# Scatter order of a weight table's tail, the place of TensorE's register loads in three look-ups, and the order of VectorE's score sums

## The chip, the cores and the metric

The program runs on one core of a Trainium2 chip. The metric is the device time of one execution in microseconds (us). Before the change three runs gave a median of 3548.18 us (3548.17 to 3554.03).

## The reference

Four graph layers over 3,125 nodes of 256 features and 50,000 edges, sorted by destination, each followed by a residual and a layer norm:

```python
edge_index = jnp.stack([src, dst])
x = _layernorm(x + _L0_gnn_ref(x, src, dst, edge_weight, ...))
x = _layernorm(x + _L1_gnn_ref(x, ..., edge_attr_3, edge_index))
x = _layernorm(x + _L2_gnn_ref(x, edge_index, ...))
x = _layernorm(x + _L3_gnn_ref(x, src, dst, ...))
```

What the change touches are two of their parts. In L0 the neighbours are summed with the edge weights, and in L1 (and the two attention layers inside L2) every edge gets a score from its two nodes:

```python
gathered = edge_weight[:, None] * x[edge_col]                        # L0
neigh = segment_sum(gathered, edge_row, num_segments=N_NODES)
...
alpha = einsum(h_src, a_src) + einsum(h_dst, a_dst)                  # L1, 8 heads of 32
enc = relu(edge_attr @ edge_W.T + edge_b).reshape(-1, H, D)
alpha = alpha + sum(enc * h_dst, axis=-1)
...
e = alpha_s[src] + alpha_d[dst]                                      # L2, 4 heads, twice
```

L3 (three dense-table sums of neighbours, each with two projections and batch norms) isn't touched.

## The kernel before

**Tiling.** The edges stand in 392 tiles of 128 (391 with edges, `EDGES_T`), four tiles to a quad, 98 quads. The nodes stand in 25 tiles of 128, and `S` = 416 steps pair an edge tile with a node tile, since a tile of sorted edges can reach over a boundary.

**First stage, to about 640 us.** L0's sum is made as a dense product. For every edge tile VectorE sums weights and counts of equal (source, destination) cells (`summed`, L2061), and GpSimd writes them into a table `t_w` in device memory with one indirect DMA for each edge tile (`weight_sums`, L803, the scatter at L817). Rows of the table are destination nodes, so row tile t is complete when the quads up to some number, read from the data into `need_i`, have landed. With some 16 edge tiles to a row tile that number is 84 for row tile 20, 88 for 21, 92 for 22, 96 for 23 and 98 for 24. The order of the scatters is `w_order` (L382): groups of eight quads, in each group first tile 0 of all its quads, then tile 1, and so on; the last group has ten quads, 88 to 97. Two scatters of the same quad must not be in flight together, so each one waits until the one eight before it has landed (`written`, L393; eight semaphores, `moved` and `gath`, in turn). As GpSimd passes such a wait it raises `w_landed` by the quads that are complete (`quads_by`, L386), and after the last scatter it waits for all that is left and raises the rest.

SyncE reads the table back, two row tiles at a time (a pair, 13 pairs), each in a left and a right half, into a ring of four buffers in SBUF: `complete` (L585) waits for `w_landed` of that row tile, L608 issues the load, and the buffer has to be free, which TensorE's `w_out` tells. TensorE turns the counts (L993) and multiplies the weights with the nodes' features (L1018); VectorE adds the pairs (L2421).

**The look-ups.** In three layers (k = 0 for L1 and k = 1, 2 for the two attention layers) TensorE's `look_up` (L1138) makes, for four steps a turn and four turns a lap, the edge's source terms by one-hot products (L1159, L1169) and the target terms by one-hot products with the table of one node tile (L1180 for k = 0, L1182 else). Which node tile belongs to a step is known only from the data: it stands in `tn_i` and is loaded into 16 registers once a lap (`tiles_at`, L1133, the load at L1135), behind the source products of turn 0. For k = 0 TensorE also makes the products of the edges' attributes (L1151), which ScalarE passes through relu (L1535); for each turn VectorE's `of_edges` (L2183) takes the maximum over the source terms, which are all but one strongly negative (L2190), copies the targets' own term (L2195), multiplies the attributes with the targets' features (L2196) and sums (L2201). A first look-up runs from about 700 to 1134 us, the second from 1631 to 1785, the third from 2228 to 2398. Beside them GpSimd gathers rows of the nodes' features (L853, L900) and puts some aside (L874); behind each, `add_up` (L1251) sums these rows with the weights (L1259), which VectorE accumulates (L2344).

Of the kernel before, what the change touches and what calls it, by code (L numbers as in the profile page):

```python
# [6 lines left out]
P = 128  # L7
N = 3125
NT = 25
# [4 lines left out]
S = ET + NT - 1  # L14
SB, SQ = 4, 104
UN, HU = 16, 8
# [24 lines left out]
D = 256  # L41
# [16 lines left out]
PIECES = WT // 2  # L58
W_GROUP = 8
HALF_W = 12 * P  # L60
STAGED = [range(0, 6), range(6, 12), range(12, 18), range(18, NT)]
# [22 lines left out]
def build(nc, a):  # L84

    with ExitStack() as ctx:
# [60 lines left out]
        drel = sb("drel", [P, S])  # L147
        tn_i = sb("tn_i", [P, S], I32)
        te_i = sb("te_i", [SQ, SB], I32)
# [231 lines left out]
        w_groups.append(range(W_GROUP * len(w_groups), QUADS))  # L381
        w_order = [L0H * q + b for quads in w_groups for b in range(L0H) for q in quads if L0H * q + b < EDGES_T]  # L382
        w_first = [min(n for n, j in enumerate(w_order) if j // L0H == quads[0]) for quads in w_groups]
        quads_by = []
        for n in range(len(w_order)):
# [4 lines left out]
            quads_by.append(q)  # L390
        quads_by.append(0)

        def written(j):  # L393
# [391 lines left out]
        def _(pool):  # L785
# [17 lines left out]
            def weight_sums():  # L803

                pool.wait_ge(*count("need", 1))
                for n, j in enumerate(w_order):
                    if n == w_first[-1]:
                        pool.wait_ge(*count("w_zero", PIECES))
                    elif n in w_first:
                        m = w_first.index(n)  # L810
                        pieces = pool.value_load(zero_i[0:1, m:m + 1], min_val=1, max_val=PIECES)
                        pool.wait_ge(done("w_zero"), pieces)
                        pool.sem_inc(done("pool_go"), 1)
                    pool.wait_ge(*count("w_summed", j // L0H + 1))
                    if n >= 2 * NACC:
                        pool.wait_ge(*written(n - 2 * NACC))
                    pool.indirect_dma_start(t_w, bass.IndirectOffsetOnAxis(ap=w_x[:, j:j + 1], axis=0), w_pair[:, j, :],  # L817
                                            None).then_inc((moved + gath)[n % (2 * NACC)], 16)
                    if n >= 2 * NACC and quads_by[n - 2 * NACC] > quads_by[n - 2 * NACC - 1]:
                        pool.sem_inc(done("w_landed"), quads_by[n - 2 * NACC] - quads_by[n - 2 * NACC - 1])  # L820
                for n in range(EDGES_T - 2 * NACC, EDGES_T):
                    pool.wait_ge(*written(n))
                pool.sem_inc(done("w_landed"), QUADS - quads_by[EDGES_T - 2 * NACC - 1])

# [89 lines left out]
        def _(pe):  # L914
# [217 lines left out]

            def tiles_at(first):  # L1133

                pe.load(tn_regs, tn_i[0:1, bass.ds(first, UN)])  # L1135
                return [pe.snap(r, min_val=0, max_val=NT - 1) for r in tn_regs]

            def look_up(k, H):  # L1138
# [4 lines left out]
                def sixteen_steps(i, half):  # L1143

                    for q in range(UN // QU):
# [25 lines left out]
                        mm.then_inc(done("src_mm"), 1)  # L1171
                        if q == 0:
                            at = tiles_at(i * UN)
                        pe.wait_ge(*count("dst_used", n + ahead))
                        if k == 0:
                            pe.wait_ge(*count("hot_s", n + 1 + UN // QU))
                        for j in range(QU):
                            hot = hot_t[:, q % 2, j * P:(j + 1) * P] if k == 0 else hot_b[:, 4 * half + q, 1, j * P:(j + 1) * P]
                            if k == 0:
                                mm = pe.matmul(ps[:, 4 + j, 0:GW], hot, hrows[:, bass.ds(at[q * QU + j], 1), :], start=True, stop=True)  # L1180
                            else:
                                mm = pe.matmul(ps[:, 2 + q % 2, 24 * j:24 * j + 24], hot, dst_b[:, bass.ds(at[q * QU + j], 1), :, :],  # L1182
                                               start=True, stop=True)
                        mm.then_inc(done("dst_mm"), 1)

                if k == 0:
                    with pe.Fori(0, S // UN) as i:
                        sixteen_steps(i, 0)
                else:
                    with pe.Fori(0, S // UN // 2) as i:  # L1190
                        for half in range(2):
                            sixteen_steps(2 * i + half, half)
# [672 lines left out]
        def _(dve):  # L1865
# [48 lines left out]
            dve.wait_ge(*count("te_ps", 2))  # L1914
            link(dve.tensor_tensor(tn_i[:, :], iota[:, 0:S], ps[:, 0, 0:S], ALU.subtract))
            link(dve.tensor_scalar(last_of, iota[0:EQ, 0:QUADS // W_GROUP - 1], float(W_GROUP), float(W_GROUP - 1), ALU.mult, ALU.add))
# [244 lines left out]
            def edge_scores(k, H):  # L2161
# [20 lines left out]

                def of_edges(i, q):  # L2183

                    n = 4 * i + q
                    now = bass.ds(i * UN + q * QU, QU)
                    mix = mixed[:, q % 2]
                    dve.wait_ge(*count("sc_dv", n + 1))
                    dve.wait_ge(*count("src_mm", n + 3))
                    dve.tensor_reduce(mix[:, :, 33].rearrange("p (b u) -> p b u", b=2), ps[:, 0:2, 0:2 * NT * H].rearrange("p b (u t) -> p b u t", t=NT),  # L2190
                                      AX.X, ALU.max).then_inc(done("src_used"), 1)
                    by_head = mix.rearrange("p (u h) w -> p u h w", u=QU)
                    dve.wait_ge(*count("enc_done", n + 3))
                    dve.wait_ge(*count("dst_mm", n + 3))
                    dve.tensor_copy(by_head[:, :, :, 32:33], ps[:, 4:8, D + 8:D + 16].unsqueeze(3))  # L2195
                    last = dve.tensor_tensor(by_head[:, :, :, 0:32], enc[:, q * QU:q * QU + QU, :].rearrange("p u (h d) -> p u h d", h=8),  # L2196
                                             ps[:, 4:8, 0:D].rearrange("p u (h d) -> p u h d", h=8), ALU.mult)
                    last.then_inc(done("dst_used"), 1)
                    dve.wait_ge(*count("src_used", n + 3))
                    dve.wait_ge(*count("dst_used", n + 3))  # L2200
                    dve.tensor_reduce(alpha[:, now, :], by_head, AX.X, ALU.add).then_inc(done("sc_dv"), 1)  # L2201

                lo_compare(0, 0)
                if k == 0:
                    with dve.Fori(0, S // UN) as i:
                        for q in range(UN // QU):
                            if q % 2 == 0:
                                lo_compare(i + q // 2, 1 - q // 2)
                            of_edges(i, q)
                else:  # L2210
                    with dve.Fori(0, S // UN // 2) as i:
                        for q in range(8):
                            if q % 2 == 0:
                                lo_compare(2 * i + (q + 2) // 4, (1 + q // 2) % 2)
                            of_nodes(2 * i + q // 4, q % 4)
# [488 lines left out]
```

## Time and profile before

| | |
|---|---|
| median of 3 runs | 3548.18 us |
| the profiled execution | 3550.85 us, its span 3549.1 us |
| TensorE matmuls busy | 2954.9 us, 83% of the span |
| VectorE busy | 2395.4 us, 67% |
| GpSimd busy | 1689.1 us, 48% |
| ScalarE busy | 1594.3 us, 45% |
| scatters, L817 | 391, 58.7 to 571.0 us, busy 378.5 us |

The profile is of one execution. Its engines are called PE (TensorE; PEld is its weight load), DVE (VectorE), ACT (ScalarE), POOL (GpSimd) and SP (SyncE); a q behind the name is the engine's instruction queue. A busy share over the whole span is an average over stages, so the rows below are taken from the stages one by one. In a row of waits "X <- Y" says that X's engine stood idle ahead of X until Y; "issue" is time in which it waited for nothing that the profile shows. Buffers have the names of the memory that they lie in, so `score_sb` or `shared_sb` is another thing in another stage.

### The profile page before, as it was taken

The numbers are of one execution on the slowest core, as the hardware profiler recorded it, in microseconds if no ns is written. First come the engines' busy times: TensorE is split into PE (matmuls) and PEld (weight loads), VectorE is DVE, ScalarE is ACT, GpSimd is POOL, SyncE is SP. The second block draws the span as 40 slices with busy tenths as digits, with TensorE's granted clock in tenths as the row PEclk, the third lists the DMA queues.
The fourth block names the chain that finished last, engine by engine and source line by source line (L and its number), as shares of the span: only waits on it lengthen the run. The fifth ranks groups of instructions, "written<-read, shape, count | busy, mean of one in ns | idle before, by whom it ended". The sixth has DMA issues, their size and how long they took to land. (4 is left out here: it accounts for less than half of the span.)

```text
span 3549.1 us, 59408 instructions
## 1 busy us (share of the span) xinstructions
PE 2954.9 (83%) x15273; PEld 1898.7 (53%) x15274; DVE 2395.4 (67%) x5420; ACT 1594.3 (45%) x3200; POOL 1689.1 (48%) x1731
## 2 busy tenths in 40 slices
PE   5999998899997698887779976677976469999996
PEld 2344444677776344386634434563434357587775
DVE  8883333488898998945799976569976763334334
ACT  3872222489997466531056655005654440410302
POOL 3777773065555775206777770676777201000000
PEclk7999999999999799978989987798997679999998
DMA  9998997289887455466811110993445233143241
GB/s 400 375 361 295 319 320 249 80 260 268 262 257 236 135 182 158 126 240 184 227 31 27 27 27 17 342 287 91 131 139 174 60 115 111 51 129 92 89 134 37
DMA packets 392782, 625.10 MB, mean 176 GB/s; under 512 B 129011, under 2 KB 274100, under 8 KB 385486
## 3 DMA queue, kind: packets, MB, share of 16 engines
q1 hardware_dynamic: 258818, 436.76, 37.1%
q0 software_dynamic: 72144, 145.54, 14.0%
q10 hardware_dynamic: 61632, 40.70, 3.6%
q8 instruction: 67, 1.10, 0.1%
q14 instruction: 121, 0.99, 0.1%
HBM read 442.67 MB, written 183.69 MB: 176 GB/s over the span
## 5 line engine op out<-in xcount | busy, mean ns | idle before, releaser
L1543 ACT ACTIVATE onehot<-iota,drel 128x128 f32<-128x128 f32 x1248 | 381.6, 388 | 681.4 <-PE ps L1259 342.8
L1259 PE MATMUL ps<-shared_sb,onehot 128*128 128x264 f32 (+1 forms) x1600 | 554.8, 444 | 92.6 <-DVE accum L2344 87.6
L2344 DVE TENSOR_TENSOR accum<-accum,ps 128x264 f32 (+1 forms) x1248 | 528.5, 423 | 9.0 <-DVE accum L2344 3.8
L1259 PEld LDWEIGHTS ps<-shared_sb,onehot 128*128 128x128 f32 x1600 | 261.4, 200 | 385.1 <-issue 238.6
L817 POOL DMA_INDIRECT t_w<-early_sb x391 | 378.5, 968 | 162.9 <-issue 94.4
L834 POOL TENSOR_SCALAR onehot<-iota,carry_d 98x512 bf16<-98x512 f32 x28 | 44.7, 1603 | 785.5 <-PE ps L1336 645.9
L1319 PE MATMUL ps<-counts_r,h_hi 128*128 128x512 f32 (+1 forms) x1050 | 321.4, 387 | 12.2 <-DVE h_lo L2606 12.2
L853 POOL DMA_INDIRECT shared_sb<-table,src_x x272 | 262.0, 963 | 112.5 <-issue 76.7
L1319 PE MATMUL ps<-counts_r,h_lo 128*128 128x512 f32 (+1 forms) x1050 | 312.4, 379 | 0.0
L853 POOL DMA_INDIRECT rows<-table,src_x x184 | 180.0, 978 | 178.3 <-DMA table<-score_sb 92.3
L2421 DVE TENSOR_TENSOR accum<-accum,ps 128x512 f32<-128x512 f32 (+1 forms) x156 | 103.9, 667 | 229.9 <-PE ps L1018 229.8
L900 POOL DMA_INDIRECT resid_sb<-table,src_x x224 | 212.4, 948 | 88.8 <-issue 57.3
L2330 DVE TENSOR_TENSOR shared_sb<-shared_sb,ps 128x256 f32<-128x256 f32 x512 | 212.6, 415 | 44.6 <-DMA shared_sb<-table,src_x 25.4
L1180 PE MATMUL ps<-score_sb,onehot 128*128 x832 | 219.7, 407 | 22.9 <-issue 20.2
L1319 PEld LDWEIGHTS ps<-counts_r,h_hi 128*128 128x128 f32 x1050 | 195.9, 190 | 54.1 <-issue 12.6
L1319 PEld LDWEIGHTS ps<-counts_r,h_lo 128*128 128x128 f32 x1050 | 193.2, 190 | 39.1
L853 POOL DMA_INDIRECT score_sb<-table,src_x x168 | 175.1, 1042 | 75.1 <-issue 46.8
L853 POOL DMA_INDIRECT resid_sb<-table,src_x x144 | 136.6, 949 | 136.0 <-DMA t_resid<-resid_sb 82.6
L1018 PE MATMUL ps<-resid_sb,score_sb 128*128 128x512 f32 (+1 forms) x364 | 188.0, 597 | 0.0
L1180 PEld LDWEIGHTS ps<-score_sb,onehot 128*128 128x128 f32 x832 | 150.6, 191 | 59.2 <-issue 29.0
L1546 ACT ACTIVATE onehot<-onehot,ones 128x1024 f32<-128x1024 f32 x156 | 179.2, 1149 | 5.1
L1169 PE MATMUL ps<-accum 128*128 128x100 bf16 x2496 | 169.6, 225 | 0.0
(441 smaller groups left out, 6061.8 us busy)
## 6 DMA issues: line engine op xcount, KB each, us to landing
t_w<-onehot SPq DMA_DIRECT2D x13, 6400.0 KB
accum<-t_hot SPq DMA_DIRECT2D x208, 256.0 KB
shared_sb<-t_adj SPq DMA_DIRECT2D x53, 640.0 KB, 10.0
resid_sb<-t_w SPq DMA_DIRECT2D x13, 1664.0 KB
t_aside<-rows POOLq DMA_DIRECT2D x40, 512.0 KB
resid_sb<-t_w SPq DMA_DIRECT2D x13, 1536.0 KB
score_sb<-t_w SPq DMA_DIRECT2D x12, 1664.0 KB
shared_sb<-t_w SPq DMA_DIRECT2D x12, 1536.0 KB
```

Source lines behind the costliest of these rows:

```text
L817: pool.indirect_dma_start(t_w, bass.IndirectOffsetOnAxis(ap=w_x[:, j:j + 1], axis=0), w_pair[:, j, :], None).then_inc((moved + gath)[n % ( ...
L853: pool.indirect_dma_start(to[:, u, 0:w], None, tab, bass.IndirectOffsetOnAxis(ap=src_x[:, step:step + 1], axis=0)).then_inc(landing[0], 16)
L900: pool.indirect_dma_start(x_rows[n % (RG[1] // HU)][:, u, :], None, table[1], bass.IndirectOffsetOnAxis(ap=src_x[:, n * HU + u:n * HU + u ...
L1018: mm = pe.matmul(ps[:, m % 6, at:at + now.stop - now.start], lhs, w_cells[2 * h + t % 2][0:EQ if t == NT else P, from_half, 0], start=(t = ...
L1169: mm = pe.matmul(out, hot, src_b8[:, m, :] if k == 0 else src_b[:, m, :, :], start=False, stop=(m == 2 and (j % 2 == 1 if k == 0 else j == ...
L1180: mm = pe.matmul(ps[:, 4 + j, 0:GW], hot, hrows[:, bass.ds(at[q * QU + j], 1), :], start=True, stop=True)
L1259: pe.matmul(ps[:, RING[(HU * h + u) % len(RING)], 0:w], onehot[:, h % 2 * HU + u, :], around[g][place(g, i, h)][:, u, 0:w], start=True, st ...
L1319: mm = pe.matmul(ps[:, 2 * (i % 3) + f, 0:w], part[:, t, f * P:(f + 1) * P], whole_counts[at % WORK][:, c, 0:w], start=(t == 0 and part is ...
L1543: last = act.activation(onehot[:, h % 2 * HU + u, :], iota[:, 0:P], ACT.Abs, bias=drel[:, bass.ds(step + u, 1)], scale=-1.0)
L1546: act.activation(onehot[:, pair, :], onehot[:, pair, :], ACT.Relu, bias=ones[:, 0:1], scale=-1.0).then_inc(oh_ready, 1)
L2330: dve.tensor_tensor(v, of_src, now_w[:, u, 0:H].unsqueeze(2).to_broadcast([P, H, D // H]), ALU.mult).then_inc(msg_ready, 1)
L2344: dve.tensor_tensor(to, to, bank.unsqueeze(1), ALU.add).then_inc(step_acc, 1)
```

## The change

It has three parts.

1. *Scatters.* From quad 80 on the groups are 80 to 83, 84 to 87, 88 to 92 and 93 to 97 (`TAIL`). With groups of four and five, two scatters of one quad stand four or five apart, so from scatter 320 on each waits for the one four before it (`landed_by`), and `w_landed` is raised by the same rule.
2. *Tile numbers.* The load of 16 registers becomes two of 8 (`tiles_in`), one behind the target products of turn 1 and one behind those of turn 3, both for the lap after; two loads stand ahead of the loop, and `tn_i` has 16 zeros more, which the last lap's loads read.
3. *VectorE's sums.* For k = 0 the sum of a turn stands behind the maximum of the turn after it; the first lap is taken out of the loop, and the last sum stands behind it.

```diff
--- before.py
+++ after.py
@@ -57,6 +57,7 @@
...
 W_GROUP = 8
+TAIL = [range(80, 84), range(84, 88), range(88, 93), range(93, 98)]
 HALF_W = 12 * P
@@ -145,7 +146,7 @@
...
         drel = sb("drel", [P, S])
-        tn_i = sb("tn_i", [P, S], I32)
+        tn_i = sb("tn_i", [P, S + UN], I32)
         te_i = sb("te_i", [SQ, SB], I32)
@@ -379,7 +380,9 @@
...
         w_groups.append(range(W_GROUP * len(w_groups), QUADS))
-        w_order = [L0H * q + b for quads in w_groups for b in range(L0H) for q in quads if L0H * q + b < EDGES_T]
+        w_turns = [quads for quads in w_groups if quads[0] < TAIL[0][0]] + TAIL
+        w_order = [L0H * q + b for quads in w_turns for b in range(L0H) for q in quads if L0H * q + b < EDGES_T]
+        tail_at = w_order.index(L0H * TAIL[0][0])
         w_first = [min(n for n, j in enumerate(w_order) if j // L0H == quads[0]) for quads in w_groups]
@@ -389,6 +392,10 @@
...
         quads_by.append(0)
+
+        def landed_by(n):
+
+            return n - (2 * NACC if n < tail_at else len(TAIL[0]))
@@ -812,15 +819,15 @@
...
                     pool.wait_ge(*count("w_summed", j // L0H + 1))
-                    if n >= 2 * NACC:
-                        pool.wait_ge(*written(n - 2 * NACC))
+                    for m in range(max(0, landed_by(n - 1) + 1), landed_by(n) + 1):
+                        pool.wait_ge(*written(m))
                     pool.indirect_dma_start(t_w, bass.IndirectOffsetOnAxis(ap=w_x[:, j:j + 1], axis=0), w_pair[:, j, :],
                                             None).then_inc((moved + gath)[n % (2 * NACC)], 16)
-                    if n >= 2 * NACC and quads_by[n - 2 * NACC] > quads_by[n - 2 * NACC - 1]:
-                        pool.sem_inc(done("w_landed"), quads_by[n - 2 * NACC] - quads_by[n - 2 * NACC - 1])
-                for n in range(EDGES_T - 2 * NACC, EDGES_T):
+                    if landed_by(n) >= 0 and quads_by[landed_by(n)] > quads_by[landed_by(n - 1)]:
+                        pool.sem_inc(done("w_landed"), quads_by[landed_by(n)] - quads_by[landed_by(n - 1)])
+                for n in range(landed_by(EDGES_T - 1) + 1, EDGES_T):
                     pool.wait_ge(*written(n))
-                pool.sem_inc(done("w_landed"), QUADS - quads_by[EDGES_T - 2 * NACC - 1])
+                pool.sem_inc(done("w_landed"), QUADS - quads_by[landed_by(EDGES_T - 1)])
@@ -1130,10 +1137,13 @@
...
-            def tiles_at(first):
-
-                pe.load(tn_regs, tn_i[0:1, bass.ds(first, UN)])
-                return [pe.snap(r, min_val=0, max_val=NT - 1) for r in tn_regs]
+            def tiles_in(half, first):
+
+                pe.load(tn_regs[half * HU:half * HU + HU], tn_i[0:1, bass.ds(first + half * HU, HU)])
+
+            def tiles_at(half):
+
+                return [pe.snap(r, min_val=0, max_val=NT - 1) for r in tn_regs[half * HU:half * HU + HU]]
@@ -1169,20 +1179,24 @@
...
                         mm.then_inc(done("src_mm"), 1)
-                        if q == 0:
-                            at = tiles_at(i * UN)
+                        if q % 2 == 0:
+                            at = tiles_at(q // 2)
                         pe.wait_ge(*count("dst_used", n + ahead))
...
                             if k == 0:
-                                mm = pe.matmul(ps[:, 4 + j, 0:GW], hot, hrows[:, bass.ds(at[q * QU + j], 1), :], start=True, stop=True)
+                                mm = pe.matmul(ps[:, 4 + j, 0:GW], hot, hrows[:, bass.ds(at[q % 2 * QU + j], 1), :], start=True, stop=True)
                             else:
-                                mm = pe.matmul(ps[:, 2 + q % 2, 24 * j:24 * j + 24], hot, dst_b[:, bass.ds(at[q * QU + j], 1), :, :],
+                                mm = pe.matmul(ps[:, 2 + q % 2, 24 * j:24 * j + 24], hot, dst_b[:, bass.ds(at[q % 2 * QU + j], 1), :, :],
                                                start=True, stop=True)
                         mm.then_inc(done("dst_mm"), 1)
-
+                        if q % 2 == 1:
+                            tiles_in(q // 2, i * UN + UN)
+
+                for half in range(2):
+                    tiles_in(half, 0)
                 if k == 0:
@@ -1912,7 +1926,8 @@
...
             dve.wait_ge(*count("te_ps", 2))
-            link(dve.tensor_tensor(tn_i[:, :], iota[:, 0:S], ps[:, 0, 0:S], ALU.subtract))
+            dve.memset(tn_i[:, S:S + UN], 0)
+            link(dve.tensor_tensor(tn_i[:, 0:S], iota[:, 0:S], ps[:, 0, 0:S], ALU.subtract))
             link(dve.tensor_scalar(last_of, iota[0:EQ, 0:QUADS // W_GROUP - 1], float(W_GROUP), float(W_GROUP - 1), ALU.mult, ALU.add))
@@ -2180,33 +2195,50 @@
...
-                def of_edges(i, q):
+                def of_sources(i, q):
...
                     n = 4 * i + q
-                    now = bass.ds(i * UN + q * QU, QU)
-                    mix = mixed[:, q % 2]
                     dve.wait_ge(*count("sc_dv", n + 1))
                     dve.wait_ge(*count("src_mm", n + 3))
-                    dve.tensor_reduce(mix[:, :, 33].rearrange("p (b u) -> p b u", b=2), ps[:, 0:2, 0:2 * NT * H].rearrange("p b (u t) -> p b u t", t=NT),
+                    dve.tensor_reduce(mixed[:, q % 2, :, 33].rearrange("p (b u) -> p b u", b=2), ps[:, 0:2, 0:2 * NT * H].rearrange("p b (u t) -> p b u t", t=NT),
                                       AX.X, ALU.max).then_inc(done("src_used"), 1)
-                    by_head = mix.rearrange("p (u h) w -> p u h w", u=QU)
+
+                def of_targets(i, q):
+
+                    n = 4 * i + q
+                    by_head = mixed[:, q % 2].rearrange("p (u h) w -> p u h w", u=QU)
                     dve.wait_ge(*count("enc_done", n + 3))
...
                     dve.tensor_copy(by_head[:, :, :, 32:33], ps[:, 4:8, D + 8:D + 16].unsqueeze(3))
-                    last = dve.tensor_tensor(by_head[:, :, :, 0:32], enc[:, q * QU:q * QU + QU, :].rearrange("p u (h d) -> p u h d", h=8),
-                                             ps[:, 4:8, 0:D].rearrange("p u (h d) -> p u h d", h=8), ALU.mult)
-                    last.then_inc(done("dst_used"), 1)
+                    dve.tensor_tensor(by_head[:, :, :, 0:32], enc[:, q * QU:q * QU + QU, :].rearrange("p u (h d) -> p u h d", h=8),
+                                      ps[:, 4:8, 0:D].rearrange("p u (h d) -> p u h d", h=8), ALU.mult).then_inc(done("dst_used"), 1)
+
+                def summed_up(i, q):
+
+                    n = 4 * i + q
                     dve.wait_ge(*count("src_used", n + 3))
                     dve.wait_ge(*count("dst_used", n + 3))
-                    dve.tensor_reduce(alpha[:, now, :], by_head, AX.X, ALU.add).then_inc(done("sc_dv"), 1)
+                    dve.tensor_reduce(alpha[:, bass.ds(i * UN + q * QU, QU), :], mixed[:, q % 2].rearrange("p (u h) w -> p u h w", u=QU),
+                                      AX.X, ALU.add).then_inc(done("sc_dv"), 1)
+
+                def edge_turns(i):
+
+                    for q in range(UN // QU):
+                        if q % 2 == 0:
+                            lo_compare(i + q // 2, 1 - q // 2)
+                        of_sources(i, q)
+                        if q > 0:
+                            summed_up(i, q - 1)
+                        elif not first_lap(i):
+                            summed_up(i - 1, UN // QU - 1)
+                        of_targets(i, q)
...
                 if k == 0:
-                    with dve.Fori(0, S // UN) as i:
-                        for q in range(UN // QU):
-                            if q % 2 == 0:
-                                lo_compare(i + q // 2, 1 - q // 2)
-                            of_edges(i, q)
+                    edge_turns(0)
+                    with dve.Fori(1, S // UN) as i:
+                        edge_turns(i)
+                    summed_up(S // UN - 1, UN // QU - 1)
                 else:
```

On GpSimd, the scatters from n = 320 on, which begin a group before and after. `moved0` to `moved3` and `gath0` to `gath3` are the eight semaphores in turn, `s_w_zero` is the zeroing of the table and `s_w_summed` the sums in SBUF. Before:

```order
L817 DMA t_w<-early_sb 10649600x2 [waits s_w_zero,moved0,s_w_summed]
L817 DMA t_w<-early_sb 10649600x2 [waits moved1,s_w_summed]
L817 DMA t_w<-early_sb 10649600x2 [waits moved2,s_w_summed]
L817 DMA t_w<-early_sb 10649600x2 [waits moved3,s_w_summed]
L817 DMA t_w<-early_sb 10649600x2 [waits gath0,s_w_summed]
```

and now:

```order
L824 DMA t_w<-early_sb 10649600x2 [waits s_w_zero,moved2,moved3,moved1,gath0,moved0,s_w_summed]
L824 DMA t_w<-early_sb 10649600x2 [waits gath1,s_w_summed]
L824 DMA t_w<-early_sb 10649600x2 [waits gath2,s_w_summed]
L824 DMA t_w<-early_sb 10649600x2 [waits gath3,s_w_summed]
L824 DMA t_w<-early_sb 10649600x2 [waits moved0,s_w_summed]
```

The semaphore that a scatter waits for was its own, raised by the scatter eight before; now it is the one four places on in the ring, raised by the scatter four before. The first of the tail catches up with five at once.

On TensorE, the first two turns of a lap of the first look-up. ISA and REGISTER_ALU are waits and register work. Before:

```order
L1151 MATMUL ps<-attr_wb,shared_sb 128x256 x4
L1155 ISA
L1159 MATMUL ps<-not_lo,lo_hot 128x400 x2
L1169 MATMUL ps<-accum,shared_sb 128x200 x12
L1135 ISA
L1135 TENSOR_LOAD tn_i
L1136 ISA x2
L1176 REGISTER_ALU
L1180 ISA
L1180 MATMUL ps<-score_sb,onehot 128x272
```

and now, from the source products of turn 0, with the target products of turn 1 behind them:

```order
L1179 MATMUL ps<-accum,shared_sb 128x200 x12
L1146 ISA
L1186 REGISTER_ALU
L1190 ISA
L1190 MATMUL ps<-score_sb,onehot 128x272
...
L1190 ISA
L1190 MATMUL ps<-score_sb,onehot 128x272
L1142 ISA
L1142 TENSOR_LOAD tn_i
L1159 REGISTER_ALU
L1161 MATMUL ps<-attr_wb,shared_sb 128x256 x4
```

Between the source and the target products no load is left; it stands behind the target products of the second turn (and, the same again, behind those of the fourth).

On VectorE, one turn of the first look-up. Before:

```order
L2190 TENSOR_REDUCE score_sb<-ps 128x32
L2195 COPY score_sb<-ps 128x32
L2196 TENSOR_TENSOR score_sb<-accum,ps 128x32x32
L2201 ISA
L2201 TENSOR_REDUCE score_sb<-score_sb 128x32
```

and now:

```order
L2203 TENSOR_REDUCE score_sb<-ps 128x32
L2221 ISA
L2221 TENSOR_REDUCE score_sb<-score_sb 128x32
L2212 COPY score_sb<-ps 128x32
L2213 TENSOR_TENSOR score_sb<-accum,ps 128x32x32
```

The sum, which stood right behind the product that it reads, is now that of the turn before and stands between the maximum and the copy.

## Rows read from the trace of the kernel before

**Rows 1.** Timeline of TensorE, 566 to 590 us: start us, us, engine, line, operation, [idle before].
```profile
568.87 0.39 PE L1018 MATMUL ps<-score_sb 128*128 128x128 f32 x2
583.17 0.27 PE L993 MATMUL ps<-ident_h,resid_sb 128*128 128x128 f16 x1 [13.92 <-issue]
...
583.56 2.02 PE L1018 MATMUL ps<-resid_sb,score_sb 128*128 128x512 f32 x2
```

**Rows 2.** Timeline of SyncE's DMA issues, 510 to 640 us.
```profile
573.30 0.32 SPq L608 DMA_DIRECT2D resid_sb<-t_w  x1
574.30 0.32 SPq L608 DMA_DIRECT2D shared_sb<-t_w  x1
```

**Rows 3.** Waits of SyncE, 250 to 640 us: us in total, times, longest us.
```profile
SPq L589 <- POOLq L823: 17.3, 1, 17.3
```

**Rows 4.** Timeline of GpSimd, 560 to 580 us.
```profile
570.96 0.96 POOL L817 DMA_INDIRECT t_w<-early_sb  x1 [0.30 <-issue]
```

**Rows 5.** Busy us by window: length, PE, PEld, DVE, ACT, POOL, granted clock, DMA share, GB/s.
```profile
500.00:550.00 50.00, 47.91 (x200) 23.23 (x200) 15.98 (x24) 13.91 (x24) 38.02 (x40) 1.00 0.92 312
550.00:600.00 50.00, 35.73 (x137) 16.72 (x136) 10.74 (x16) 9.34 (x16) 16.75 (x18) 0.86 0.58 209
...
800.00:850.00 50.00, 48.85 (x333) 38.75 (x331) 45.71 (x60) 47.97 (x52) 29.55 (x32) 1.00 0.88 273
...
2230.00:2280.00 50.00, 36.07 (x476) 29.50 (x474) 28.16 (x94) 0.00 (x0) 34.46 (x37) 0.80 1.00 323
```

**Rows 6.** Waits of the first look-up, 720 to 1130 us.
```profile
PEld ps L1180 <- issue: 25.9, 25, 2.0
DVE score_sb L2201 <- DVE score_sb L2196: 23.5, 100, 0.2
...
ACT accum L1535 <- PE ps L1151: 19.7, 24, 1.8
DVE score_sb L2195 <- PE ps L1180: 18.8, 24, 1.8
...
PEld ps L1159 <- DVE score_sb L2190: 4.9, 23, 0.7
```

**Rows 7.** Timeline of TensorE, 852.5 to 858.5 us.
```profile
852.30 1.08 PE L1180 MATMUL ps<-score_sb,onehot 128*128 x4
...
856.40 2.10 PE L1180 MATMUL ps<-score_sb,onehot 128*128 x8 [1.19 <-issue]
```

**Rows 8.** Line 1135's loads: ns min/median/max, whole span; then 850 to 860 us.
```profile
L1135 PEldq TENSOR_LOAD <-tn_i x78: 1102/1110/3919, 707.3 to 2393.3; - x78
...
L1135 PEldq TENSOR_LOAD <-tn_i x1: 1888/1888/1888, 853.8 to 853.8; - x1
```

**Rows 9.** Waits of GpSimd, 110 to 571 us.
```profile
POOL t_w L817 <- DMA t_w<-early_sb: 22.0, 69, 1.3
```

**Rows 10.** Timeline of GpSimd, 1068 to 1081 us.
```profile
1074.12 0.95 POOL L853 DMA_INDIRECT rows<-table,src_x  x1 [0.30 <-issue]
...
1080.54 0.79 POOL L874 DMA_DIRECT2D t_aside<-rows  x1 [4.60 <-DMA rows<-table,src_x]
```

**Rows 11.** Line 2335's register loads, of 8 each, on VectorE: ns min/median/max.
```profile
L2335 DVEq TENSOR_LOAD <-tn_i x156: 593/597/850, 1191.2 to 2786.2; - x156
```

**Rows 12.** Waits of GpSimd, 1186 to 1500 us.
```profile
POOL onehot L834 <- PE ps L1259: 47.2, 1, 47.2
```

**Rows 13.** Waits from 1630 to 2150 us.
```profile
PEld ps L1182 <- issue: 31.4, 26, 1.3
...
DVE shared_sb L2330 <- DMA resid_sb<-table,src_x: 19.4, 10, 3.5
```

**Rows 14.** Waits from 2220 to 2440 us.
```profile
PEld ps L1182 <- issue: 36.1, 26, 3.3
DVE lo_hot L2167 <- DMA lo_w<-t_lo: 36.0, 27, 4.0
...
POOL score_sb L853 <- PE ps L1259: 16.2, 1, 16.2
```


## The prediction

> **What bounds the kernel now.** I read the page's busy shares first: no engine is the bound of the whole span, so each of the three parts of the change has to be priced in its own stage. For the first stage (to about 640 us) I took SyncE's timeline, its waits, then TensorE's and GpSimd's timelines at one place. The reader is to see this. TensorE ends pair 10 at 568.87 and starts pair 11 only at 583.17, a hole of 13.92 us, with the next products at 2.02 us a pair of matmuls [rows 1]. The loads of pair 11's two row tiles are issued at 573.30 and 574.30 [rows 2]; SyncE had waited 17.3 us for the last signal of the scatters [rows 3]; the last scatter starts at 570.96 and nothing but the table's writes is between it and 573.30 [rows 4]. So the end of the 391 scatters sets the restart of TensorE, about 14 us of lost time.
>
> For the first look-up (about 700 to 1134) I took the table by windows: TensorE 48.85, ScalarE 47.97 and VectorE 45.71 of 50 us, all three close to full [rows 5]. The list of waits of that stage then shows what is left over: TensorE's weight loads before the target products idle 25.9 us in 25 places, ScalarE waits 19.7 us for TensorE in 24, VectorE 18.8 us in 24 [rows 6]. There are 26 laps, so this is one event per lap; on TensorE's timeline the hole stands ahead of the target products (1.19 us, released by "issue") [rows 7], and in that lap the register load took 1888 ns [rows 8]. It is the load of the 16 tile numbers.
>
> **The change part by part.** My sum is made against the profiled execution, 3550.85 us; the median of the runs is 3548.18, 2.67 lower, so 2.67 comes off at the end. A measurement of this kernel can tell about 0.2%, 7.1 us, from no change.
>
> *Scatters.* Quads 80 to 97 (71 scatters, n = 320 to 390) now go in groups of four and five, and each waits for the one four before it, not eight. What is removed: tile 22's rows need 92 quads, which are complete with n = 370 (passed by n = 374) where it was n = 385, passed only behind the last scatter, so of the two tiles only tile 23 still waits for the end. What is added: a wait that binds once a scatter takes longer to land than four starts. Starts stand 0.96 + 0.30 = 1.26 us apart [rows 4], so four are 5.04 us and eight were 10.1. No view gives the landing of a scatter, so I bound it. From below: the last one, with nothing else on the DMA engines, started at 570.96 and let SyncE issue at 573.30, at most 2.3 us [rows 2, 4]. From above: from 110 to 571 us the wait for eight back was never longer than 1.3 us, of which 0.3 is the usual gap, so about 11 us at the most [rows 9]. Nearest rows: GpSimd's gathers, also indirect DMAs of 128 rows, at a DMA share of 0.87 to 0.88. The last gather of a run starts at 1074.12 and the copy that waits for it goes at 1080.54: 6.4 us [rows 10, 5]. In the tail the share is 0.92 up to 550 us [rows 5]. I take 6.0, somewhat below the gather because a scatter carries fewer bytes. Pace then 6.0 / 4 = 1.50 us, and 71 x (1.50 - 1.26) = +17 us at the drain. Against that, one tile instead of two is loaded behind it: before, 583.17 - 573.30 = 9.9 us from issue to restart for two tiles, half of that would be 5, I take 6, so -4. **+13 us.** The ends: -4 (landing below 5.04), +20 (landing 6.4 throughout: 71 x 0.34 = 24, less 4). While GpSimd stands in such a wait nothing else is queued there but more scatters; SyncE, which waits for the signal ahead of its other loads, and TensorE behind it, stand too. The load of tile 21 (its last quad is complete with n = 351, which n = 359 waited for, at 570.96 - 31 x 1.26 = 532, and now n = 355: n = 320 starts at 483, and 35 x 1.5 behind that is 535) is late as well, but that delay runs into the same hole and isn't counted twice. The extra SyncE work is none: same loads, same order.
>
> The Trainium skill, "DMA: Bandwidth & Descriptors", section "Anatomy of one DMA — SWDGE (gpsimd) path", puts a GpSimd DMA at a constant 2.0 us plus its bytes at the engines' rate; by that a scatter would land in 2 us whatever else runs, four starts would be ample, and the sum for this part would be -4 instead of +13. The idle-DMA scatter (2.3 us at most) agrees with it, the gather's 6.4 us under load doesn't.
>
> *Tile numbers.* One load of 16 registers a lap (median 1110 ns, up to 3919 [rows 8]) between the source and target products becomes two of 8, each behind target products whose numbers are already there, for the lap after. Loads of 8 registers of the same table stand in VectorE's queue: 597 ns median, 850 at most [rows 11]. What hides one is TensorE's sequencer running ahead of its matmuls: in the lap of rows 7 it lost 1.19 us of a 1.89 us load, so its lead there was 0.7 us. 0.6 us fits in such a lead; behind four target products (1.08 us for the four, longer than the source products) it should not be shorter. What can come back is bounded by the co-bound engines, not by TensorE: ScalarE's 19.7 us of waits are about all its idle time here (50 - 47.97 = 2.0 of each 50 us, 17 over 430 us). I take **-17 us** for the first look-up, the rest of the 19.7 being what slow loads and the loop branch still expose. Ends: -21 (ScalarE's waits and a bit) and -4 (the load half exposed at both places: 52 x 0.3 = 16 us returned). After the look-up nothing swallows this: in 1186 to 1500 GpSimd itself waits 47.2 us for TensorE's sums [rows 12].
>
> The second look-up (1631 to 1785) gets the same edit, and there I cost the gain at nothing: the gathers run back to back over it, and the sums behind it wait for them (19.4 us on VectorE [rows 13]); time won moves into those waits. If that cover were gone, the 31.4 us in 26 places that TensorE loses to the loads there would be the most to win [rows 13]. The third (2228 to 2398) runs at a DMA share of 1.00 in its first part [rows 5], and VectorE waits 36.0 us for its own DMA [rows 14]; GpSimd's gathers stop once, 16.2 us, until TensorE starts its sums [rows 14]. That is the most that can come back there; the transfers set the pace of much of the stage, so of the 36.1 us that TensorE loses to the loads [rows 14] I let at most that 16.2 through and take somewhat under half of it: **-7 us**, ends -16 and 0.
>
> *VectorE's order.* The sum of turn n-1 now stands behind the source maximum of turn n. That takes out the 23.5 us (100 times 0.2) in which the sum waited for its own product [rows 6]. VectorE is not the last of the three (45.71 against 47.97), so this pays nothing by itself; and one reduction falls behind the loop. **0**; a gain is excluded while the other two are fuller, and the other end is +5: TensorE waits 4.9 us for the source maximum already [rows 6], and that could double where the maximum, held up itself, now also holds up a sum that was ready.
>
> The zeros behind the table and two loads ahead of the loop: under 2 us, off the path while VectorE and SyncE prepare. Sum: 13 - 17 - 7 = -11, so 3539.85 in the profiled execution and **3537 us** on the median's scale.
>
> **The rivals.**
> 1. The scatters land within 5.04 us. For it: the idle scatter of 2.3 us. Against: the gathers under load. Then -4 - 17 - 7 = -28: **3520**. The rule of the Trainium skill's "DMA: Bandwidth & Descriptors" named above is this case.
> 2. The ring of four becomes the bound for good: slower. If a scatter lands in 7.5 us while tile loads and table stores run, the pace is 1.875, 71 x 0.61 - 4 = +39 on the restart of pair 11, and 39 - 24 = +15: **3563**. It decides from 71 x (L/4 - 1.26) - 4 > 24 + 7, that is L above 7.0 us. For it: rows 9 allow up to 11, and TensorE has no other work in that hole. Against: the gathers of rows 10 are below it, and the load is lighter behind 550 us (share 0.58 in 550 to 600 [rows 5]).
> 3. The look-ups give back half: the 8-register loads stay half exposed, or VectorE's new order costs what they save. 13 - 9 - 3 = +1: **3549**. For it: loads of up to 3.9 us in rows 8 say that some are held up, and two chances to be held up replace one.
>
> **How the numbers follow.** Chances: forecast 0.42, rival 1 0.16, rival 2 0.14, rival 3 0.28. The forecast's own range is 3529 to 3546 (the ends of its terms, not all at once); "faster" is below 3541.1, "slower" above 3555.3. Of the forecast 0.30 lies in faster and 0.12 in same; rival 1 all in faster (0.16); rival 2 all in slower (0.14); rival 3 0.02 faster, 0.22 same, 0.04 slower. So faster 0.48, same 0.34, slower 0.18. The range takes in rival 1 nearly whole and the near part of rival 2: 3518 to 3560.
>
> **What would show it.** Right: scatters of the tail 1.4 to 1.6 us apart, with GpSimd waiting for the table's writes; the last about 587; tile 22's load some 20 us ahead of tile 23's; TensorE's hole before pair 11 longer, 24 to 29 us; the load's hole gone from the target products of look-up one and ScalarE's wait for TensorE under 5 us there; GpSimd's single 16.2 us wait in the third look-up about half. Wrong: tail scatters still 1.27 us apart (rival 1), or 1.8 and more (rival 2); holes ahead of the products of the second and fourth turn of a lap (rival 3); a second look-up whose gain reaches the sums, which would make it faster than I say.

## The result, and the profile after the change

| | before | after |
|---|---|---|
| median of 20 runs | 3548.44 us | 3553.28 us |
| lowest to highest | 3545.16 to 3557.94 | 3549.40 to 3559.83 |
| ratio | | 1.0013 (95%: 1.0007 to 1.0018) |
| the profiled execution, its span | 3550.85, 3549.1 | 3551.16, 3549.3 |

The change makes the kernel 0.13% slower, some 5 us. The forecast was 3537 and 11 us faster: the time lies inside the range (3518 to 3560), the sign is wrong. The two profiled executions are as long as each other only by chance: the one of before lies 2.4 us above its median, the one after 2.1 below.

**First stage.** GpSimd's waits from 480 to 600 us, then the end of its timeline (start, us, engine, line, operation, [idle before]):

```profile
POOL t_w L824 <- DMA t_w<-early_sb: 28.2, 18, 3.3
POOL t_w L824 <- issue: 18.6, 55, 1.4
```

```profile
589.82 0.96 POOL L824 DMA_INDIRECT t_w<-early_sb  x1 [0.30 <-issue]
591.09 0.96 POOL L824 DMA_INDIRECT t_w<-early_sb  x1 [0.30 <-issue]
595.34 0.96 POOL L824 DMA_INDIRECT t_w<-early_sb  x1 [3.30 <-DMA t_w<-early_sb]
```

Before, from 500 to 575 us, none of the waits for the table's writes was longer than the usual gap of 0.3 us:

```profile
POOL t_w L817 <- DMA t_w<-early_sb: 4.0, 13, 0.3
```

Now the 18 waits put down to them take 28.2 us; 5 of these are the usual gap, and 13 take 0.9 to 3.3 each. The last scatter starts at 595.34 where it was 570.96 [rows 4], 24.4 us later. SyncE's issues, its wait for the last signal, and TensorE's restart:

```profile
567.28 0.32 SPq L615 DMA_DIRECT2D resid_sb<-t_w  x1
597.69 0.32 SPq L615 DMA_DIRECT2D shared_sb<-t_w  x1
```

```profile
SPq L596 <- POOLq L830: 28.9, 1, 28.9
```

```profile
604.38 0.27 PE L1000 MATMUL ps<-ident_h,resid_sb 128*128 128x128 f16 x1 [29.40 <-issue]
```

Tile 22 is loaded 30 us ahead of tile 23, as the change means it to be, and behind the last signal one tile takes 6.7 us to TensorE's restart (597.69 to 604.38) where two took 9.9. But the signal is 24.4 us late, and the hole grows from 13.92 [rows 1] to 29.40; TensorE restarts at 604.38 where it was 583.17, 21.2 us later (pair 10 too ends 5.7 us later, at 575.0).

**First look-up.** Waits from 720 to 1160 us (us in total, times, longest), and the register loads (ns min/median/max):

```profile
DVE lo_hot L2182 <- DMA lo_w<-t_lo: 23.4, 22, 2.3
PEld ps L1190 <- issue: 22.6, 40, 1.3
PEld ps L1161 <- issue: 14.9, 19, 7.0
...
ACT accum L1549 <- PE ps L1161: 9.5, 15, 1.2
ACT score_sb L1542 <- DMA accum<-t_drel: 9.3, 15, 1.8
```

```profile
L1142 PEldq TENSOR_LOAD <-tn_i x162: 587/593/2047, 721.6 to 2398.8; - x162
```

The load is now 593 ns, as read from VectorE's [rows 11], and ScalarE's wait for TensorE is halved, from 19.7 [rows 6] to 9.5. New in their place are waits for transfers: 23.4 us for `lo_w` and 9.3 for `t_drel`, the values from which VectorE and ScalarE make one-hots. Either took 1.0 in the same view of before:

```profile
DVE lo_hot L2167 <- DMA lo_w<-t_lo: 1.0, 2, 0.6
ACT score_sb L1528 <- DMA accum<-t_drel: 1.0, 1, 1.0
```

By windows (us, then busy PE, PEld, DVE, ACT, POOL, granted clock, DMA share, GB/s), before and after:

```profile
755.00:855.00 100.00, 97.71 (x671) 77.59 (x669) 91.45 (x115) 95.91 (x104) 66.08 (x71) 1.00 0.87 261
855.00:955.00 100.00, 91.93 (x627) 72.89 (x624) 86.73 (x109) 90.85 (x97) 52.97 (x57) 1.00 0.89 264
955.00:1055.00 100.00, 95.75 (x651) 75.89 (x651) 89.03 (x114) 92.97 (x100) 52.95 (x57) 1.00 0.88 257
```

```profile
755.00:855.00 100.00, 100.00 (x684) 80.81 (x682) 92.46 (x119) 98.55 (x106) 70.59 (x75) 1.00 0.89 265
855.00:955.00 100.00, 95.29 (x648) 75.54 (x646) 87.16 (x112) 93.51 (x100) 53.77 (x59) 1.00 0.90 265
955.00:1055.00 100.00, 93.39 (x628) 73.71 (x628) 85.46 (x110) 91.39 (x97) 51.20 (x56) 1.00 0.93 264
```

After the change TensorE has no gap at all in the first 100 us; then it loses 5 to 7 of 100, while DMA moves the same 265 GB/s, and is hardly better off than before (8 and 4). From its first to its last target product the look-up takes 416.3 us; before it took 418.9.

**Third look-up.** Waits of GpSimd, 2220 to 2440 us:

```profile
POOL rows L860 <- DMA table<-score_sb: 91.5, 1, 91.5
...
POOL score_sb L860 <- DMA score_sb<-table,src_x: 2.0, 3, 1.4
POOL score_sb L860 <- PE ps L1273: 1.3, 1, 1.3
```

Of the 16.2 us for TensorE's sums [rows 14] 1.3 are left, not half.

### The profile page after: what moved, and what is told of

Same layout as the page of the kernel before. It is cut to its first block and busy times, and to the rows that moved or that the text cites. A ratio compares the mean times of both kernels' runs of the same rounds, so it can differ in the third digit from the quotient of the medians.

```text
span 3549.3 us, 59587 instructions
## 1 busy us (share of the span) xinstructions
PE 2937.0 (83%) x15273; PEld 1885.4 (53%) x15274; DVE 2387.5 (67%) x5421; ACT 1595.4 (45%) x3200; POOL 1684.3 (47%) x1731
## 5 line engine op out<-in xcount | busy, mean ns | idle before, releaser
L841 POOL TENSOR_SCALAR onehot<-iota,carry_d 98x512 bf16<-98x512 f32 x28 | 44.8, 1605 | 782.6 <-PE ps L1350 644.5
L1169 PE MATMUL ps<-not_lo,lo_hot 128*128 128x400 bf16 x416 | 129.1, 351 | 97.9 <-DVE score_sb L2189 54.9
```

Of the source, the lines that this page charges most:

```text
L1169: pe.matmul(ps[:, b if k == 0 else q % 2, 0:n_to * NT * H], lo_hot[:, q, :], not_lo[:, to, :].unsqueeze(2).to_broadcast([P, n_to, H, NT]), ...
```

## The experiments

Each kernel has a ratio to runs of the kernel before on the same chip, with its 95% interval. Stage times are from the first to the last target product on TensorE's timeline.

**e1, e2, e3, e4: the parts alone.** e1 has the hunks of `TAIL`, `w_order`, `landed_by` and `weight_sums` alone, e2 those of `tn_i`, `tiles_in` and `look_up`, e3 those of VectorE's `edge_scores`, e4 the last two together.

> Only the new scatter order and its wait for four back. Theory 1 (the ring of four costs, and the delay reaches the end): the pair stage ends some 21 us later, as in the whole change (658.8 against 637.4), and the total is 15 to 22 us slower than before (GpSimd's back-to-back gathers may take up a few us). Rival (the delay is taken up by later waits, and what holds the whole change back is elsewhere): the pair stage ends 21 us later, the total is within 7 us of before.

> Only the two loads of 8 registers behind the target products. Theory 1 (the loads give what the change gives back, VectorE's order nothing): the hole ahead of the first target products of a lap is gone, the first look-up is 7 to 11 us shorter, the total 12 to 18 us faster. Rival (the loads pay only together with VectorE's new order): laps of 15.5 us or more in the first look-up, total less than 8 us faster.

> Only VectorE's order in the first look-up. Theory 1 (VectorE is not the last of the three engines there): within 4 us of before, the hole at the register load as before. Rival (the new order itself is what shortens the laps): 5 us or more faster. Second rival (it holds up sums that were ready): 5 us or more slower.

> The whole change without the scatters. Theory 1: the parts add up, so about 16 us faster than before (the whole change is 5 slower, the scatters cost 21). Rival (the look-ups are held by transfers, and what they gain is lost again wherever the scatters don't delay them): less than 8 us faster.

| | median | ratio (95%) | in us |
|---|---|---|---|
| e1, scatters | 3571.93 | 1.0062 (1.0049 to 1.0075) | +22 |
| e2, loads | 3529.25 | 0.9948 (0.9936 to 0.9959) | -18 |
| e3, sums | 3549.11 | 1.0002 (0.9991 to 1.0013) | 0 |
| e4, loads and sums | 3531.54 | 0.9953 (0.9940 to 0.9966) | -17 |

(In us: ratio less 1, times 3546.51, the median of before beside them.) The parts add up: +22 - 17 is the 5 us of the whole. In e1 the pair stage's last product starts at 658.1 (before 637.5) and the delay of 21 us is still there at the end. VectorE's order is worth nothing alone or with the loads. e2 and e4 both beat both kernels; between the two the intervals don't tell. One half of e2's first theory failed: its total came as expected, but its first look-up takes 419.1 us, no shorter than before.

**e5: the old order, only the wait shortened.**

```diff
-TAIL = [range(80, 84), range(84, 88), range(88, 93), range(93, 98)]
+TAIL = [range(80, 88), range(88, 98)]
...
-            return n - (2 * NACC if n < tail_at else len(TAIL[0]))
+            return n - (2 * NACC if n < tail_at else 4)
```

(against e1)

> The kernel before with the scatters in their old order, and only the wait from scatter 320 on shortened from eight back to four back. Theory 1 (the shorter wait is what costs): the last scatter starts some 20 to 25 us later than 571, with GpSimd waiting for the table's writes, and as two tiles are still loaded behind it the total is 20 to 28 us slower. Rival (the new order costs, by tile 22's load among the scatters): the last scatter within 5 us of 571, total within 7 us of before.

Measured: 1.0060 (1.0043 to 1.0076), +21 us. GpSimd's waits from 480 to 620 us and its last scatter:

```profile
POOL t_w L824 <- DMA t_w<-early_sb: 23.6, 18, 2.9
POOL t_w L824 <- issue: 18.9, 55, 1.2
```

```profile
590.25 0.95 POOL L824 DMA_INDIRECT t_w<-early_sb  x1 [0.30 <-issue]
```

Nearly as many long waits (11 of 0.9 us or more, against 13), a last scatter 19.3 us later (20 to 25 were expected), and the same loss, without the new order. So the wait for four back is what costs, and what the new order brings (one tile behind the signal) is not seen beside it.

**e6: five from quad 88 on.** The whole change, with

```diff
-TAIL = [range(80, 84), range(84, 88), range(88, 93), range(93, 98)]
+TAIL = [range(88, 93), range(93, 98)]
```

> The whole change, but the tail begins at quad 88 (groups 88 to 92 and 93 to 97), and each of its 39 scatters waits for the one five back. Theory 1 (a wait binds where a scatter lands later than the starts that it spans, 5 x 1.26 = 6.3 us here): half the scatters are under it, a stall is shorter by one start, so the drain is 6 to 12 us later than before and not 24, less 3 for the one tile: about 3 to 9 us worse than the loads and sums alone, 7 to 14 us faster than before. Rival (every ring below eight costs about the same): no faster than before.

Measured: 0.9963 (0.9951 to 0.9976), -13 us; 4 us behind e4, within 3 to 9 as theory 1 has it, though the two intervals overlap. GpSimd's waits from 480 to 620 us, SyncE's issues of pair 11 and TensorE's restart:

```profile
POOL t_w L824 <- issue: 17.2, 56, 0.4
POOL t_w L824 <- DMA t_w<-early_sb: 9.0, 17, 1.7
```

```profile
553.51 0.32 SPq L615 DMA_DIRECT2D resid_sb<-t_w  x1
579.09 0.32 SPq L615 DMA_DIRECT2D shared_sb<-t_w  x1
```

```profile
585.39 0.27 PE L1000 MATMUL ps<-ident_h,resid_sb 128*128 128x128 f16 x1 [20.53 <-issue]
```

The signal comes 5.8 us after that of before (579.09 against 573.30 [rows 2]), one tile then takes 6.3 us, and TensorE restarts 2.2 us later than before. Even where the ring costs only 6 us, the early load of tile 22 doesn't pay for it.

**e7, e8: the first look-up without its neighbour.** GpSimd's put-asides, gathers and stores beside most of that look-up, wait until it has ended; e7 is the kernel before, e8 is e2 with the same hold.

```diff
-                    if g in ASIDE and n == (8 if g == 0 else 0):
-                        put_aside()
                     if g == 0 and n == 8:
                         looked_up()
+                    if g in ASIDE and n == (8 if g == 0 else 0):
+                        put_aside()
```

> The kernel before, with GpSimd's put-asides, which run beside most of the first look-up, held back until it has ended; the total is not the point. Theory 1 (transfers disturb the laps): from about 800 us on the look-up's laps are all 15.65 us, with one load of 16 registers each, and the look-up takes 405 to 415 us instead of 424. Rival (the register loads alone make the long laps): it stays at 420 or more.

> The same hold with the two loads of 8 registers. Theory 1 (what the loads win in the first look-up is lost to transfers that come late): laps of 15.2 to 15.3 us all through, look-up 395 to 405 us, that is 8 to 12 us shorter than with the hold and the old load, where without the hold it was 1 to 3 us. Rival (something on the engines holds it): no shorter than with the hold and the old load.

Measured: the look-up takes 408.0 us in e7 and 396.3 in e8, 11.7 less (the whole kernels, one execution each, 3761.91 and 3739.41, since the put-asides then come late). Two windows of e7, then the same of e8:

```profile
855.00:955.00 100.00, 97.71 (x662) 77.70 (x663) 91.26 (x117) 95.48 (x103) 0.00 (x0) 1.00 0.57 152
955.00:1055.00 100.00, 97.71 (x670) 77.72 (x668) 91.44 (x116) 96.00 (x103) 0.00 (x0) 1.00 0.59 153
```

```profile
855.00:955.00 100.00, 100.00 (x690) 79.42 (x688) 93.64 (x119) 98.58 (x106) 0.00 (x0) 1.00 0.60 159
955.00:1055.00 100.00, 100.00 (x686) 79.53 (x684) 93.41 (x119) 98.66 (x106) 0.00 (x0) 1.00 0.64 156
```

Waits from 850 to 1100 us in e7:

```profile
PEld ps L1180 <- issue: 9.8, 16, 0.7
ACT accum L1535 <- PE ps L1151: 7.3, 16, 0.5
```

With the DMA share at 0.6 and not 0.9, from about 850 us on the laps are 15.64 to 15.72 us with one load of 16 (the last 15.91) and 15.20 with two of 8. The hold takes GpSimd's own work away too; but VectorE's and ScalarE's instructions take as long without it as beside it (VectorE's sum 1286 ns in e7 and in before, ScalarE's relu 1022 in both), so what it takes out are waits. Two things follow. A load that isn't held up costs 0.45 us a lap, 26 laps 11.7 us; and ScalarE's 7.3 us in 250 are some 12 over the look-up: of the 19.7 that I took for the load's alone [rows 6], the rest came with the transfers beside it, which delay other things when the load is gone.

**e9, e10: which look-up pays.** e2 with the new loads for some k alone, the load of 16 as before for the others:

```diff
+                        if q == 0 and k not in (2,):
+                            all_tiles(i * UN)
...
-                        if q % 2 == 1:
+                        if q % 2 == 1 and k in (2,):
                             tiles_in(q // 2, i * UN + UN)
...
-                for half in range(2):
+                for half in range(2 if k in (2,) else 0):
                     tiles_in(half, 0)
```

(e9 against e2; e10 has `(0, 1)`)

> The two loads of 8 registers in the third look-up alone; the first two keep the load of 16, scatters and sums as before. Theory 1 (the third look-up gives nearly all that comes back): third look-up 156 to 160 us instead of 170, total 12 to 17 us faster than before. Rival (the parts of the look-ups add up, the third gives 7 as predicted): 5 to 9 us faster.

> The two loads of 8 registers in the first and second look-up, the third with the load of 16. Theory 1: the first gives 1 to 3 us, held by transfers, and the second's 9 us are lost again in the sums behind it: total within 4 us of before. Rival (the first look-up gives the predicted 17, less what single traces show by chance): 10 us or more faster.

Measured: e9 0.9952 (0.9939 to 0.9966), -17 us; e10 0.9982 (0.9971 to 0.9994), -6 us. The third look-up gives most of it (it takes 160.3 us in e9, just above the 156 to 160 expected). The first two together give 2 to 10 by the interval, between what theory and rival had. In all traces here without the hold the first look-up takes 412.5 to 421.7 us with the old load (before, e1, e3, e5, e9) and 416.3 to 425.5 with the new (after, e2, e4, e6, e10), so its own spread is as large as what is asked. Some 3 us can be placed ahead of it, where these times don't reach: the first target product starts 11.0 us behind the last product of the stage before in all six kernels with the new loads there, and 13.7 to 14.1 behind it in the six without. Where the rest of e10's 6 us comes from is open. The second look-up is plainly shorter (141.4 to 142.4 us; 151.4 to 152.5 in before, e1, e3 and e5, 147.1 in e9), and gives it back in the sums behind it. VectorE's waits in these, 1800 to 2143 us of e4:

```profile
DVE shared_sb L2355 <- DMA resid_sb<-table,src_x: 19.4, 9, 3.4
DVE shared_sb L2355 <- DMA early_sb<-table,src_x: 17.9, 10, 2.3
DVE shared_sb L2355 <- issue: 10.7, 37, 0.6
DVE shared_sb L2355 <- DMA shared_sb<-table,src_x: 3.9, 3, 2.1
```

The first is as before (19.4 [rows 13]); of the others, `early_sb` had 11.7 and `shared_sb` 0.3 in the view of before, from 1630 to 2150 us. The sums take 342.1 us of TensorE's timeline where they took 333.1.

## Why the prediction was wrong, point by point

- **Scatters, forecast +13, ends -4 and +20: measured +22 (e1).** The mechanism was the one forecast: the wait for four back binds, GpSimd stands, SyncE and TensorE behind it stand too, and nothing later takes it up. The size was off, in the step "I take 6.0, somewhat below the gather because a scatter carries fewer bytes". The tail of the changed kernel, from 484.05 on, ran at (595.34 - 484.05) / 70 = 1.59 us a scatter, which by my own division is a landing of 6.4, the gather's, and gives the upper end, +20. The row was the price; the discount on it had no row behind it. It doesn't come evenly either, but as 13 stalls of 0.9 to 3.3 us with mostly the old rhythm of 1.26 between them. The terms for the tile were right (6.7 us against the 6 taken). Of the signs, the last scatter was to start about 587 and started at 595.3; the hole was to be 24 to 29 us long and was 29.4.
- **The constant 2.0 us.** The Trainium skill's "DMA: Bandwidth & Descriptors", section "Anatomy of one DMA — SWDGE (gpsimd) path", which was rival 1, is out here: with it no wait for four back could have been long, and e1 has 12 and e5 11 of 0.9 us or more.
- **First look-up, forecast -17, ends -21 and -4: measured nothing that its spread lets be told, and 3 us ahead of it.** The step that failed is "What can come back is bounded by the co-bound engines". The bound was not on the list of engines. The row had DMA share 0.88 [rows 5] and I used it only to price scatters. e7 and e8 show it: with the transfers out of the way the loads are worth 11.7 us, with them nothing that can be told. Even undisturbed they are worth less than the 17, since part of ScalarE's 19.7 us was the transfers' too; its wait, which was to fall under 5 us, is 9.5. "After the look-up nothing swallows this" was not put to the test, as the look-up gave nothing to swallow.
- **Second look-up, forecast 0.** Right, and for the reason given: 9 to 10 us shorter, and the sums behind it 9 us longer (e4).
- **Third look-up, forecast -7, ends -16 and 0: about -14 us in the look-up (156.2 in e4, 170.4 before), -17 in e9's total.** The step that failed is "the transfers set the pace of much of the stage". A DMA share of 1.00 was not a limit: the same 50 us, at nearly the same place of the look-up, move more with the new loads (e4):

```profile
2230.00:2280.00 50.00, 33.13 (x502) 28.06 (x502) 31.00 (x104) 0.00 (x0) 36.14 (x39) 0.87 1.04 359
```

  against 323 GB/s [rows 5]. And the ceiling that I had named, GpSimd's single wait of 16.2 us, was what came back: it is gone in e4, and in e9 this is left of it:

```profile
POOL score_sb L853 <- PE ps L1272: 2.2, 1, 2.2
```

  What the sum didn't have at all is TensorE's clock; the last section has its rows.

- **VectorE's order, forecast 0.** Right (e3), since TensorE and ScalarE were fuller.
- **The sum.** Forecast 13 - 17 - 7; by the runs +22, and -17 of which the third look-up is most. The gain as a whole was forecast 7 us too large, the cost 9 too small, and most of the gain was put in the wrong look-up; these 16 us are what turned the sign. Of the rivals, the third came nearest, in time (3549) and in that a look-up gives back what it gains, but through transfers and not through the loads or VectorE.

## What to carry to other kernels

Shortening the distance at which an indirect DMA waits for an earlier one turned latency into rate here (1.26 us a scatter became 1.59); price such a change by a landing under the load of that place, undiscounted, and not by one on idle queues. When a stall is taken out of a stage where engines and DMA are all near nine tenths, ask which transfer is late next: it may be the one that had made the stall long. A single long wait of an engine that otherwise runs nearly without a gap was here the best bound for a gain upstream of it (GpSimd's 16.2 us, and 17 that came back in e9).

## What the runs showed that I had not expected

**The clock of the second and third look-up.** Over the third look-up, from its first to its last target product, before and in e4:

```profile
2227.70:2398.10 170.40, 125.60 (x1755) 103.22 (x1755) 106.24 (x357) 0.00 (x0) 123.29 (x130) 0.85 0.96 309
2223.90:2380.20 156.30, 110.44 (x1758) 93.65 (x1756) 106.70 (x359) 0.00 (x0) 112.51 (x119) 0.92 0.98 326
```

TensorE's idle time is as long in both (44.8 and 45.9 us): ahead of the target products it is gone, but ahead of the source products TensorE now stands as much longer, mostly for VectorE. What is 15 us less is its busy time for the same products, at a mean granted clock of 0.92 of full speed (2.4 GHz; the lower level is 1.2) where it was 0.85. All six traces with the load of 16 in this look-up have 0.77 to 0.87, and it takes 169 to 177 us; all six with two loads of 8 have 0.92 to 0.95, and it takes 156 to 160. The second look-up divides in the same way (0.90 to 0.92, and 0.98 to 0.99), while the windows of the first have 1.00 before and after. TensorE's timeline of before shows what a load can do, in the third look-up:

```profile
2267.65 0.70 PE L1169 MATMUL ps<-accum 128*128 128x100 bf16 x12
2270.79 0.63 PE L1182 MATMUL ps<-accum 128*128 x4 [2.45 <-issue]
...
2271.74 1.20 PE L1169 MATMUL ps<-accum 128*128 128x100 bf16 x12
...
2274.40 0.70 PE L1169 MATMUL ps<-accum 128*128 128x100 bf16 x12
```

Twelve source products take 0.70 us ahead of the hole of 2.45 us, 1.20 behind it, and 0.70 again two turns later, so this hole cost more than its own length. How much of the third look-up's gain is the clock's, and how much the transfers', no run separates.

**Share and landing.** A DMA share of 1.00 or 1.04 is no rate: the same stretch read 323 GB/s before and 359 in e4, and GpSimd's gathers went on at about the same pace (37 and 39 in it). And a scatter can land late with the DMA engines idle. The wait of 3.30 us ahead of the last scatter of the changed kernel falls into this window:

```profile
590.00:595.00 5.00, 0.00 (x0) 0.00 (x0) 0.00 (x0) 0.00 (x0) 1.74 (x2) 0.50 0.02 1
```

The scatter that it waited for had started four before, at 587.30, so it took some 7.7 us on engines that moved 1 GB/s; e1 shows the like (2.82 us ahead of its last scatter), and e5 a wait of 2.86 us that ends at 583.93, though there other transfers still ran beside the start of the scatter that it waited for (576.33), to about 577. What held these scatters is open; it was not tried.
